# Value product of a decoder's self-attention: one float32 product, or three float32r products with operands in high and low parts

## What is computed

```python
q = (xn @ Wq).reshape(b, n, h, dh).transpose(0, 2, 1, 3)
kv = xn @ Wkv
k, v = (kv[..., :dh], kv[..., dh:])
q = q * cos + _rotate_half(q) * sin
k = k * cos + _rotate_half(k) * sin
sim = jnp.einsum('bhid,bjd->bhij', q, k)      # scaled, causal
attn = jax.nn.softmax(sim, axis=-1)
out = jnp.einsum('bhij,bjd->bhid', attn, v)
return out.transpose(0, 2, 1, 3).reshape(b, n, h * dh) @ Wo
```

## Time and profile before

| what | us |
|---|---|
| median of three runs | 1404.06 (1402.78 to 1408.01) |
| the profiled execution | 1405.16 |
| its span, first to last instruction | 1403.3 |
| TensorE busy | 1383.5 |
| VectorE busy | 975.1 |
| ScalarE busy | 716.2 |
| GpSimd busy | 437.1 |

### The profile page before, as it was taken

The page is one execution under the profiler, slowest core; times in us unless marked ns, Lnnn a source line. Parts: engine busy times, 40 slices in busy tenths (PEclk is TensorE's granted clock), DMA queues, the critical chain, the costliest instruction groups (busy, mean ns, idle before and its releaser), DMA issues.

```text
span 1403.3 us, 55347 instructions
## 1 busy us (share of the span) xinstructions
PE 1383.5 (99%) x25185; PEld 1169.1 (83%) x25185; DVE 975.1 (69%) x1824; ACT 716.2 (51%) x940; POOL 437.1 (31%) x433
## 2 busy tenths in 40 slices
PE   8999999999999999999999999999999999999997
PEld 6788888876788888888888888888888888888884
DVE  5776677666246768677777768677777767676766
ACT  3545445443455555555465555555465555555450
POOL 4333233222223233323333233323323233324310
PEclk9999999999999999999999999999999999999999
DMA  9100000000211121211212121211212121211100
GB/s 255 37 1 32 1 31 1 31 1 2 68 53 49 33 76 51 60 50 47 65 32 66 33 78 50 61 50 47 65 32 65 32 79 50 61 50 47 50 4 8
DMA packets 38923, 66.78 MB, mean 48 GB/s; under 512 B 3717, under 2 KB 36930, under 8 KB 38690
## 3 DMA queue, kind: packets, MB, share of 16 engines
q1 hardware_dynamic: 38690, 63.24, 15.7%
HBM read 61.40 MB, written 1.84 MB: 45 GB/s over the span
## 4 chain that ended last, share of the span: by engine, by line
PE 72%; DVE 2%; issue 0%; POOL 0%; DVEq 0%
PE proj_ps L1366 20%; PE proj_ps L1357 20%; PE score_ps L1384 14%; PE sum_ps L1409 13%; PE side_ps L1444 2%; PE side_ps L1458 1%; PE side_ps L1426 1%; PE side_ps L1451 1%; DVE amax L1245 0%; DVE hidden L1267 0%; DVE sig L1277 0%; DVE hidden L1278 0%; PE side_ps L1433 0%; DVE exps L1167 0%; DVE totals L1189 0%
## 5 line engine op out<-in xcount | busy, mean ns | idle before, releaser
L1119 ACT ACTIVATE exps<-score_ps 125x1792 f32<-125x1792 f32 x192 | 320.4, 1669 | 431.1 <-PE score_ps L1384 431.1
L1167 DVE TENSOR_SCALAR exps<-exps,top 125x896 f32<-125x896 f32 x384 | 288.1, 792 | 22.1 <-ACT exps L1119 17.5
L1384 PE MATMUL score_ps<-spread,keys 32*125 32x112 f32 x6144 | 219.0, 279 | 0.0
L1158 DVE COPY vals<-proj_ps 125x512 f32<-125x512 f32 x192 | 129.5, 688 | 116.6 <-PE proj_ps L1366 114.3
L1409 PEld LDWEIGHTS sum_ps<-exps,vals 125*32 125x32 f32 x12288 | 162.4, 110 | 46.9 <-issue 34.0
L1384 PEld LDWEIGHTS score_ps<-spread,keys 32*125 32x125 f32 x6144 | 184.8, 183 | 15.4 <-issue 0.3
L1409 PE MATMUL sum_ps<-exps,vals 125*32 125x56 f32 x12288 | 190.9, 214 | 0.0
L1049 POOL TENSOR_TENSOR low<-raw_early,high 128x500 fp32r<-128x500 f32 x64 | 84.5, 1322 | 216.8 <-PE proj_ps L1357 215.9
L1111 ACT ACTIVATE keys<-proj_ps,b_k 128x500 f32<-128x500 f32 x192 | 129.9, 677 | 23.7 <-PE proj_ps L1357 20.3
L1049 POOL TENSOR_TENSOR low_early<-raw_early,high_early 128x500 fp32r<-128x500 f32 x62 | 89.4, 1459 | 168.8 <-PE proj_ps L1357 168.8
L293 POOL TENSOR_TENSOR swapped<-swapped,sin 128x448 f32<-128x448 f32 (+1 forms) x72 | 86.0, 1198 | 126.5 <-ACT swapped L530 125.5
(11 more groups left out here) (169 smaller groups left out, 2415.2 us busy)
## 6 DMA issues: line engine op xcount, KB each, us to landing
raw_early<-in_ctxT SPq DMA_DIRECT2D x64, 500.0 KB, 4.1
raw<-in_ctxT SPq DMA_DIRECT2D x32, 500.0 KB, 3.6
w_q<-in_attn_Wq SPq DMA_DIRECT2D x4, 512.0 KB, 8.6
w_o<-in_attn_Wo SPq DMA_DIRECT2D x1, 2048.0 KB, 21.7
out<-y_out SPq DMA_DIRECT2D x16, 112.0 KB, 2.7
rows<-in_x SPq DMA_DIRECT2D x1, 1344.0 KB, 17.4
raw_early<-in_ffn_gate_wT SPq DMA_DIRECT2D x1, 1024.0 KB, 9.4
raw_early<-in_ffn_val_wT SPq DMA_DIRECT2D x1, 1024.0 KB, 5.1
```

The lines of the kernel that those rows point to most:

```text
L1119: nc.scalar.activation(exps[t % 2][:, :, :, :].rearrange("p h r n -> p r h n"), score_ps[0:TILE, :, 0:2 * QW].rearrange("p r (h n) -> p r ...
L1158: nc.vector.tensor_copy(vals[r][:, 2 * q:2 * q + 2, :, 0:HD], proj_ps[q][0:TILE, :].rearrange("p (k h d) -> p k h d", k=2, d=HD))\
L1167: nc.vector.tensor_scalar(tile, tile, LIMIT_LO, top[:, n, at:at + 1], ALU.max, ALU.min)\
L1384: ins = nc.tensor.matmul(score_ps[0:TILE, r, to:to + HE * S], keys[c % 2][32 * r:32 * r + 32, k, (at + half) * TILE:(at + half + 1) * TILE ...
```

## The change

The product becomes three products in float32r (`F32R`), accumulated in the same bank: high part of the values by high part of the probabilities, high by low, low by high. ScalarE's copies now write the high parts (`values_h`, `probsT_h`), rounded to float32r by the write; VectorE subtracts these from what is in PSUM and writes the low parts: `probs_low(p, k)`, a new step, and a subtraction at the head of `cosines` for a keys' unit. The products wait for the low part, which comes last. In VectorE's list `probs_low(p, 0)` stands ahead of `residual(p - 1)` and `probs_low(p, 1)` behind the rotation of more[2]; in pair 0 the rotation of more[2] stands ahead of both.

The new tensors take room. `w_f` and `mask_i` move into the room of `w_q` and are loaded after the last projection, with the second context chunk behind them; `w_xo` and five rows of weights and biases are held and loaded in the second stage, behind its first chunk, with waits on them in the second stage. The clearing of `w_xo` by GpSimd goes.

```diff
 def cosines(name):
                 if name[0] == "kv":
+                    dve.wait_ge(v_high, g + 1)
+                    nc.vector.tensor_tensor(values_l[g % 2][:, :, :].rearrange("p k n -> p (k n)"), bank(name)[:, D:2 * D],
+                                            values_h[g % 2][:, :, :].rearrange("p k n -> p (k n)").bitcast(F32),
+                                            ALU.subtract).then_inc(v_ready, 1)
                     dve.wait_ge(v_ready, g + 1)
...
+            def probs_low(p, k):
+
+                dve.wait_ge(probsT_high, 2 * p + k + 1)
+                nc.vector.tensor_tensor(probsT_l[k][:, :, :, :],
+                                        turn_ps[:, :, :].rearrange("p u (h s) -> p u h s", h=2)[:, :, :, 0:S],
+                                        probsT_h[k][:, :, :, :].bitcast(F32), ALU.subtract).then_inc(probsT_ready, 1)
...
+                if p == 0:
+                    for name in more[2:3]:
+                        rotary(name)
+                probs_low(p, 0)
                 if p:
                     residual(p - 1)
-                for name in more[2:3]:
-                    rotary(name)
+                    for name in more[2:3]:
+                        rotary(name)
+                probs_low(p, 1)
                 if p:
                     norm2_rows(p - 1)
...
 def probs_out(p, k):
-                nc.scalar.copy(probsT[k][:, :, :, :],
-                               turn_ps[:, :, :].rearrange("p u (h s) -> p u h s", h=2)[:, :, :, 0:S]).then_inc(probsT_ready, 1)
+                nc.scalar.copy(probsT_h[k][:, :, :, :],
+                               turn_ps[:, :, :].rearrange("p u (h s) -> p u h s", h=2)[:, :, :, 0:S]).then_inc(probsT_high, 1)
...
 def out_heads(p, k):
-                for b in range(2):
-                    ins = nc.tensor.matmul(out_ps[:, b, 0:AU * S], values[g % 2][SP * b:SP * b + SP, j, :],
-                                           probsT[k][SP * b:SP * b + SP, :, :, :].rearrange("p u h s -> p (u h s)"),
-                                           start=True, stop=True)
+                terms = [(values_h, probsT_h), (values_h, probsT_l), (values_l, probsT_h)]
+                for n, (v, w) in enumerate(terms):
+                    for b in range(2):
+                        ins = nc.tensor.matmul(out_ps[:, b, 0:AU * S], v[g % 2][SP * b:SP * b + SP, j, :],
+                                               w[k][SP * b:SP * b + SP, :, :, :].rearrange("p u h s -> p (u h s)"),
+                                               start=(n == 0), stop=(n == 2))
...
             sp.wait_ge(raw_used, 3)
-            for c in range(2):
-                sp.dma_start(early.ring(c), context_chunk(dram, c)).then_inc(early_ctx_in[c], 16)
+            sp.dma_start(early.ring(0), context_chunk(dram, 0)).then_inc(early_ctx_in[0], 16)
+            sp.wait_ge(unit_filled, UNIT[("q", GROUPS - 1, AU - 1)] + 1)
+            for k, name in enumerate(("xattn_WkT", "xattn_WvT")):
+                sp.dma_start(early.w_f[:, k, :, :], dram[name].rearrange("(c p) n -> p c n", p=P)).then_inc(early_w_in, 16)
+            sp.dma_start(early.mask_i, dram["mask"]).then_inc(early_in, 16)
+            sp.dma_start(early.ring(1), context_chunk(dram, 1)).then_inc(early_ctx_in[1], 16)
...
             load(2, 0, 2)
+            late = ((w_xo[:, :, :], dram["xattn_WoT"].rearrange("(a p) n -> p a n", p=P)),
...
+            for to, of in late:
+                sp.dma_start(to, of).then_inc(late_in, 16)
```

More of the change, by code:

```diff
@@ L47 @@
 TOTALS = (2, 6, 10)
-N_EARLY = 14
+N_EARLY = 8
+N_LATE = 6
 WEIGHTS_AT = 13
@@ L114, in block_a @@
         w_q = sb("w_q", [P, DC, AH * DH])
+        early.share(w_q[:, :, :].rearrange("p c n -> p (c n)"))
         w_kv = sb("w_kv", [P, DC, 2 * DH])
@@ L143, in block_a @@
         keyT = [sb(f"keyT{n}", [P, GROUP, S]) for n in range(2)]
-        values = [sb(f"values{n}", [P, GP, DH]) for n in range(2)]
+        values_h = [sb(f"values_h{n}", [P, GP, DH], F32R) for n in range(2)]
+        values_l = [sb(f"values_l{n}", [P, GP, DH], F32R) for n in range(2)]
         qT = [sb(f"qT{n}", [P, AU, GROUP, 2, SP]) for n in range(2)]
@@ L149, in block_a @@
         sums = sb("sums", [P, AU, 2])
-        probsT = [sb(f"probsT{n}", [P, AU // 2, 2, S]) for n in range(2)]
+        probsT_h = [sb(f"probsT_h{n}", [P, AU // 2, 2, S], F32R) for n in range(2)]
+        probsT_l = [sb(f"probsT_l{n}", [P, AU // 2, 2, S], F32R) for n in range(2)]
         outT = sb("outT", [P, AH, ROWS])
@@ L189, in block_a @@
         rot_ready = sem("rot_ready")
+        v_high = sem("v_high")
         v_ready = sem("v_ready")
+        probsT_high = sem("probsT_high")
         scores_done = sem("scores_done")
@@ L262, in _ @@
                 if n == 0:
-                    for k, name in enumerate(("xattn_WkT", "xattn_WvT")):
-                        sp.dma_start(early.w_f[:, k, :, :], dram[name].rearrange("(c p) n -> p c n", p=P))\
-                          .then_inc(early_w_in, 16)
-                    sp.wait_ge(early_zero, 2)
+                    sp.wait_ge(early_zero, 1)
                     for to, of in early.loads(dram):
@@ L284, in _ @@
             nc.gpsimd.memset(early.b_v[:, :], 0.0).then_inc(early_zero, 1)
-            nc.gpsimd.memset(early.w_xo[:, :, :], 0.0).then_inc(early_zero, 1)
             pool.wait_ge(ones_set, 2)
@@ L533, in swap @@
                     g = name[1]
-                    nc.scalar.copy(values[g % 2][:, :, :].rearrange("p k n -> p (k n)"), bank(name)[:, D:2 * D])\
-                      .then_inc(v_ready, 1)
+                    nc.scalar.copy(values_h[g % 2][:, :, :].rearrange("p k n -> p (k n)"), bank(name)[:, D:2 * D])\
+                      .then_inc(v_high, 1)
             def exps(p):
@@ L831, in __init__ @@
         self.w_l = sb("w_l", [P, 2, DC, D], F32R)
-        self.w_f = sb("w_f", [P, 2, DC, D])
         self.high = sb("high_early", [P, DC, CHUNK], F32R)
@@ L837, in __init__ @@
         self.head_of = sb("head_of", [P, HE])
-        self.mask_i = sb("mask_i", [TILE, BATCH, BT], I32)
         self.top = sb("top", [TILE, BATCH, BT])
@@ L841, in __init__ @@
         self.b_v = sb("b_v", [P, HG // 2])
-        self.w_xo = sb("w_xo", [P, HG // 2, D])
         self.part = sb("part", [P, 2])
@@ L845, in __init__, with share @@
         self.res = sb("res", [ROWS, 1])
-        self.ln_gamma = sb("ln_gamma", [ROWS, D])
-        self.ln_beta = sb("ln_beta", [ROWS, D])
-        self.gate_b = sb("gate_b", [ROWS, HID])
-        self.val_b = sb("val_b", [ROWS, HID])
-        self.out_b = sb("out_b", [ROWS, D])
+    def share(self, room):
+        n = 2 * DC * D
+        self.w_f = room[:, 0:n].rearrange("p (k c n) -> p k c n", k=2, c=DC)
+        self.mask_i = room[0:TILE, n:n + BATCH * BT].bitcast(I32).rearrange("p (b t) -> p b t", b=BATCH)
     def ring(self, n):
@@ L855, in loads @@
     def loads(self, dram):
-        pairs = [(self.mask_i[:, :, :], dram["mask"]),
-                 (self.b_k[:, :], dram["xattn_bk"]),
+        pairs = [(self.b_k[:, :], dram["xattn_bk"]),
                  (self.head_of[:, :], dram["c_head_of"]),
@@ L861, in loads @@
                  (self.res[:, :], dram["xattn_rs"].partition_broadcast(ROWS)),
-                 (self.ln_gamma[:, :], dram["xattn_gamma"].partition_broadcast(ROWS)),
-                 (self.ln_beta[:, :], dram["xattn_beta"].partition_broadcast(ROWS)),
-                 (self.gate_b[:, :], dram["ffn_gate_b"].partition_broadcast(ROWS)),
-                 (self.val_b[:, :], dram["ffn_val_b"].partition_broadcast(ROWS)),
-                 (self.out_b[:, :], dram["ffn_out_b"].partition_broadcast(ROWS))]
-        pairs += [(self.b_v[:, :], dram["xattn_bv"]), (self.part[:, :], dram["c_part"]),
-                  (self.w_xo[:, :, :], dram["xattn_WoT"].rearrange("(a p) n -> p a n", p=P))]
-        assert len(pairs) == N_EARLY
+                 (self.b_v[:, :], dram["xattn_bv"]), (self.part[:, :], dram["c_part"])]
+        assert len(pairs) == N_EARLY - 1
         return pairs
@@ L902, in set_up @@
         dve.wait_ge(loaded, 16 * N_EARLY)
-        chain(nc.vector.tensor_scalar(self.top[:, :, :], self.mask_i[:, :, :], 0.5, LIMIT_HI, ALU.is_gt, ALU.mult))
+        chain(nc.vector.tensor_scalar(self.top[:, :, :], self.mask_i, 0.5, LIMIT_HI, ALU.is_gt, ALU.mult))
         chain.inc(nc.vector.tensor_scalar(self.top[:, :, :], self.top[:, :, :], LIMIT_LO, None, ALU.add))
```

21 lines of the change are left out of this document (18 added, 3 removed).

## The result

The changed kernel takes 1432.99 us (1431.52 to 1434.03); the kernel before, run beside it, 1404.69. The ratio is 1.0198, with an interval of 1.0176 to 1.022: slower by 28 us, where 22 were forecast. The profiled execution took 1432.96 us, of which 1431.2 are the span. First its head and its row of busy times, to lay against the earlier trace rows.

What follows compares the result with a forecast made beforehand. TensorE, busy 99% of the span, was taken as the bound; 12.6 (stall) + 3.0 (keys and values) + 5.1 (first pair) + 1.2 (last two pairs) = 21.9 us on the 1404.06 median gave 1426.0 us, range 1412 to 1439.

Steps and rivals of the forecast that it cites:

- The product, 0.80 us: TensorE's three-term float32r product, both batches overlapping, takes 0.80 us instead of 0.95, 0.15 less.
- rival (a): Float32r products of different row groups don't overlap: 1.41 us a product instead of 0.80, 1437.6 us in all; chance 0.13.
- The stall before the second product: Pairs 1 to 13: TensorE waits 1.27 us for VectorE's queued second subtraction; 0.97 us net a pair, 12.6 us.
- Rival (d): The stall is about half as long, as GpSimd or VectorE close up better: 1414 us; chance 0.08.
- rival (b): VectorE's second norm waits for GpSimd's sine product, TensorE for 0.7 us in 13 pairs: 1435.1 us; chance 0.12.
- Keys and values: Even pairs 2 to 12: the values' subtraction ahead of the keys' rotation delays TensorE's output rows, 6 x 0.5 = 3.0 us.
- The first pair: Pair 0: rotation ahead of the first subtraction delays products 3.9 us, plus 1.2 at half clock speed; 5.1 us together.
- The last two pairs: Pairs 14 and 15: no projection covers the subtractions, each adding 0.7 us; 0.6 a pair, 1.2 us.
- The late loads: Loads moved after the last projection and into the second stage stay hidden: 0 us, at most 2.
- wrong if the second stage is longer: Sign against the prediction, which expected the second stage to keep its length.
- Rival (c): The second subtraction is not held back and TensorE keeps its 4.8 us gain: 1399.3 us; chance 0.06.

Runs made afterwards that it cites:

- product_alone: Changed kernel, low parts subtracted only in pair 0 and the first two groups, stale later; pair 0 in the other pairs' order: 1403.12 us, ratio 0.9985.
- low_ahead: Changed kernel with VectorE's second subtraction moved ahead of the third projection's sum qT in pairs 1 to 15: 1418.66 us, ratio 1.010.
- power_behind: Changed kernel with the third projection's sine product put ahead of the residual's power in GpSimd's queue: 1425.99 us, ratio 1.0143.
- all_moved: Changed kernel with the moves of low_ahead and values_behind together, and pair 0 in the order of the other pairs: 1406.08 us, ratio 1.0012.
- sine_later: Changed kernel with GpSimd's first sine product of even pairs from 2 waiting until less_max is done: 1425.14 us, ratio 1.0147.
- values_behind: As values_later, but GpSimd's values subtraction stands behind the sine products of the next even pair's first two projections: 1423.01 us, ratio 1.013.
- last_plain: As all_moved, but pairs 14 and 15 keep the earlier single float32 product in each half, without subtraction: 1405.72 us, ratio 1.0006.
- values_later: Changed kernel with the values copied in float32 by ScalarE and their low part made by GpSimd behind the keys' sine product: 1431.07 us, ratio 1.018.

## Why the prediction was right, and where its sum was off

It said 1426.0 in 1412 to 1439, and slower; it is 1432.99. Step by step:

- **The product, 0.80 us.** 0.81 measured: the third term starts 0.20 us behind the second (226.42 after 226.22), the second 0.31 behind the first and the turn 0.30 behind the third, so some 0.2 stands beside the columns, as assumed. The row groups overlap in float32r as in float32, so rival (a) falls. The gain without the preparation, 0.29 a pair in product_alone, is what two times 0.15 says.
- **The stall before the second product.** Forecast 1.27, measured 1.15 (4.06 against the 2.91 of low_ahead), and the product 1.01 later instead of 1.12, so 0.87 a pair instead of 0.97. The chain through residual, power, sine product and sum was the right one: low_ahead cut its last link and power_behind its middle, and each shortened the distance by what its link costs. Rival (d), half the stall, falls.
- **The second norm and GpSimd, rival (b).** The norm started at 229.84 and the sine product at 230.07; the norm took 0.40, and nothing was lost. The rival named the right mechanism and the wrong place. The slack of 0.5 us that the walk gave the norm held only while TensorE stalled: without the stall, in low_ahead and all_moved, TensorE waits for it.
- **Keys and values: the mis-sized term.** The prediction took "a chain with no slack: 0.5 us per time". The subtraction's own part measured 0.45. The step that failed is that everything behind it only moves by as much. Moved by that, less_max's third step came to stand 0.08 us behind GpSimd's sine product instead of 0.38 ahead of it, and took 0.91 longer. The two starts were in the trace of before, 198.65 and 199.03: a shift of 0.45 was larger than the lead of 0.38. Six times 0.86 is 5.2 of the 6.0 us that were missing. sine_later and values_behind show it, one by removing the meeting alone, the other by turning it around. The Trainium skill (SBUF — State Buffer, "SBUF: two separate sides") states the rule that was cited for rival (b): whoever starts first has the shared ports for its whole instruction, and a VectorE step with two SBUF inputs takes part in that. The trace agrees: VectorE's step, 1.09 us when alone, ends 0.95 after GpSimd's (216.22 against 215.27), while by_cos at 230.15, which reads PSUM, keeps its 0.62 beside the sine product of 230.07.
- **The first pair.** 5.1 forecast, 4.95 measured, and the agreement of the sum is luck. The idle time before the product is as forecast (3.69, where some 3.8 was said). But TensorE came to it 0.70 us sooner than before (43.76 against 44.46), for reasons not traced, so the product is 2.80 later instead of 4.0. Against that, the lower clock lasted 6.8 us where some 3.2 was expected, and the rest of the pair lost 2.15 instead of some 1.1. In four of the kernels with this order it lasted 3.4 us and the pair was 1.2 shorter.
- **The last two pairs.** 1.2 forecast, 1.85 measured; last_plain gives it back, with the projection's cover absent as the cause.
- **The late loads.** Nothing, as forecast: up to 1006 us into it, the second stage runs as before to within 0.02 us. The 1.57 us near its end are 3.4 us at the lower clock. They appear in the changed kernel and, at the same place of the stage, in all_moved, and not in the seven other kernels with the same late loads that leave the second stage at 1041.1 to 1041.2 (last_plain at 1041.5). The instructions there are the same in all of them. TensorE's idle of 1.45 us some 2 us earlier is there in all of them too (1396.66 in the changed kernel, 1370.42 before). What decides it was not found, and with one trace of each kernel it can't be put down to a kernel. The sign "wrong if the second stage is longer" did come true by these 1.57 us, but not by way of the loads.
- **Rival (c), the subtraction hidden.** It said 1399.3 where the subtraction comes in time. In all_moved it does for the products of pairs 1 to 13, and the time is 1406.1; without any subtraction, in product_alone, it is 1403.1. So the 4.8 us of gain were nearly right for the pairs by themselves (13 x 0.29 and more). With the subtraction in place the second norm takes 2.6 of them back, and the last pairs 1.9.

## What to carry to other kernels

A faster instruction on the busiest engine is worth its own saving at most, here 0.14 us for each of 32 products; the preparation that it needs is paid where it stands in an in-order queue, and exchanging it with the instruction that waits there for another engine took away nearly half of the loss. Taking away one wait shows the next: a slack that was counted while the engine stalled has to be counted again without the stall. Before an instruction is put into a queue, look in the trace for pairs of VectorE and GpSimd instructions behind it that start within the added time of each other: which of them starts first can decide more than the added work. And a queue's walk has to ask of each later step not only when it starts but beside what.

## What the runs showed of the hardware

- A GpSimd step that reads SBUF and a VectorE step with two inputs from SBUF hold each other up, and the one that starts first keeps its time. Started 0.08 us late, VectorE's step took 2.00 instead of 1.09; started 0.05 late, the keys' sum took 0.92 instead of 0.39; where VectorE was 0.38 ahead, GpSimd's took 1.70 instead of 1.14. by_cos, with one input from PSUM, kept its 0.62 beside a sine product.
- Float32r matmuls of 64 rows in two row groups overlap: 0.20 us for each two of 448 columns, and some 0.2 a product that doesn't go with the columns.
- After 3.68 or 3.69 us of idle on TensorE the granted clock was at 1.2 GHz, in six traces of six: for 3.4 us in four of them, for 6.8 in two. After 1.40 us at the same place it stayed at 2.4 GHz, in four of four. It also fell for 3.4 us at one place of the second stage in two of the eleven traces, with the same instructions, and cost 1.6 us there, and once for 3.4 us behind the last pair (values_later), where it cost 1.3.
